# TensorE's program filled up to whole blocks of 256 instructions in every pair of heads, with the first pair and one transposition in another order

## The reference

```
x = x + attention(layernorm(x), ctx)      # 32 heads of 128, additive position bias, mask over keys
x = x + ffn(layernorm(x))                 # base linear + LoRA of 8 experts weighted by a softmax router
attention: q = xn @ Wq; k = ctx @ Wk; v = ctx @ Wv            # 1024 x 512 by 512 x 4096 each
           p = softmax(q k^T / sqrt(128) + bias, masked)      # per batch and head, 64 x 64
           out = concat(p v) @ Wo                             # 1024 x 4096 by 4096 x 512
```

## Time and profile before

| | us |
|---|---|
| three runs | 796.79, 797.21, 797.59 (median 797.21) |
| profiled execution | 795.04 |
| its span | 793.3 |
| TensorE busy | 778.4 |
| VectorE (DVE) busy | 523.3 |
| ScalarE (ACT) busy | 399.9 |
| GpSimd (POOL) busy | 184.9 |

### The profile page before, as it was taken

The page is one execution under the profiler, slowest core; times in us unless marked ns, Lnnn a source line. Parts: engine busy times, 40 slices in busy tenths (PEclk is TensorE's granted clock), DMA queues, the critical chain, the costliest instruction groups (busy, mean ns, idle before and its releaser), DMA issues.

```text
span 793.3 us, 16707 instructions
## 1 busy us (share of the span) xinstructions
PE 778.4 (98%) x6360; PEld 652.7 (82%) x6360; DVE 523.3 (66%) x951; ACT 399.9 (50%) x1138; POOL 184.9 (23%) x203
## 2 busy tenths in 40 slices
PE   9999999999999999889999999999999999999998
PEld 7888888888888888768888888888888888887886
DVE  6883626267677666477767776677667676657974
ACT  5663525245555555555664466545654466436520
POOL 0225041033433334232211221212211221000200
PEclk9999999999999999999999999999999999999999
DMA  6536773244645547473563356435553455442002
GB/s 226 198 121 220 224 247 135 110 137 159 193 162 157 179 143 225 155 233 118 160 183 112 107 164 183 130 113 159 161 164 117 120 160 175 109 115 85 1 5 103
DMA packets 108077, 118.38 MB, mean 149 GB/s; under 512 B 44239, under 2 KB 77007, under 8 KB 107998
## 3 DMA queue, kind: packets, MB, share of 16 engines
q1 hardware_dynamic: 107998, 117.31, 47.4%
HBM read 81.64 MB, written 35.65 MB: 148 GB/s over the span
## 4 chain that ended last, share of the span: by engine, by line
PE 95%; DVE 2%; issue 1%; ACT 1%; DMA 0%; ACTq 0%
PE pY L1391 42%; PE pP L1391 40%; PE pY L1547 4%; PE pO L1572 2%; PE pT_ L1572 1%; PE pO L1391 1%; PE pT_ L1557 1%; PE pS L1557 1%; PE pS L1572 1%; ACT pr L757 1%; DVE st L977 1%; PE pS L1437 0%; PE pO L1437 0%; DVE y L1126 0%; PE pY L1464 0%
## 5 line engine op out<-in xcount | busy, mean ns | idle before, releaser
L757 ACT ACTIVATE pr<-pr,mx 128x64 f32<-128x64 f32 x256 | 86.2, 343 | 29.7 <-DVE mx L1143 29.7
L1126 DVE TENSOR_TENSOR y<-y,pY 128x512 f32<-128x512 f32 x124 | 84.5, 681 | 23.9 <-PE pY L1391 23.6
L1391 PE MATMUL pY<-wo_hi,oT_hi 128*128 128x512 f32 x248 | 97.0, 391 | 0.5 <-issue 0.5
L1391 PE MATMUL pY<-wo_lo,oT_hi 128*128 128x512 f32 x248 | 96.7, 390 | 0.0
L1391 PE MATMUL pY<-wo_hi,oT_lo 128*128 128x512 f32 x248 | 96.6, 389 | 0.0
L907 DVE TENSOR_TENSOR wk_lo<-wk_raw,wk_hi 128x256 fp32r<-128x256 f32 x96 | 49.3, 514 | 61.6 <-ACT wk_hi L649 60.4
L1391 PE MATMUL pP<-xo_hi,wk_hi 128*128 128x512 f32 x210 | 83.5, 398 | 4.1 <-DVE stage L928 2.1
L649 ACT CAST wk_hi<-twk 128x256 fp32r<-128x256 f32 x128 | 50.8, 409 | 65.1 <-PE pP L1391 54.7
L1391 PE MATMUL pP<-xo_lo,wk_hi 128*128 128x512 f32 x210 | 81.9, 390 | 0.0
L1391 PE MATMUL pP<-xo_hi,wk_lo 128*128 128x512 f32 x210 | 81.9, 390 | 0.0
L582 POOL TENSOR_TENSOR bias<-bias,madd 128x512 f32<-128x512 f32 x32 | 41.1, 1300 | 151.4 <-DMA bias<-in_fside_Bx32xSxS 151.4
(11 more groups left out here) (282 smaller groups left out, 1882.0 us busy)
## 6 DMA issues: line engine op xcount, KB each, us to landing
v_hbm<-stage SPq DMA_DIRECT2D x64, 256.0 KB, 2.3
k_hbm<-stage SPq DMA_DIRECT2D x64, 256.0 KB, 3.6
k<-k_hbm SPq DMA_DIRECT2D x16, 1024.0 KB, 5.3
v<-v_hbm SPq DMA_DIRECT2D x16, 1024.0 KB, 7.0
wk_raw<-in_L_xattn_Wk SPq DMA_DIRECT2D x16, 512.0 KB, 4.5
wo_raw<-in_L_xattn_Wo SPq DMA_DIRECT2D x16, 512.0 KB, 3.6
bias<-in_fside_Bx32xSxS SPq DMA_DIRECT2D x128, 64.0 KB, 3.5
wk_raw<-in_L_xattn_Wq SPq DMA_DIRECT2D x16, 512.0 KB, 4.7
```

Of the source, the lines that this page charges most:

```text
L757: nc.scalar.activation(pr[s][:, b, :], pr[s][:, b, :], ACT.Exp, bias=mx[:, s, b:b + 1], accum_out=sm[:, s, b:b + 1]).then_inc(exp_made, 1)
L1126: nc.vector.tensor_tensor(y[:, t, :], y[:, t, :], src[:, :], ALU.add).then_inc(y_added, 1)
L1391: mm = nc.tensor.matmul(bank_, a, b, start=first and n == 0, stop=last and n == len(terms) - 1, skip_group_check=read_between)
```

## The change

QB = QA + 1 gets a name. Block QB uses the alternating banks too, and the blocks after it use pP. The first products of QB are issued before product 4 of QA, product 1 of block QB + 1 is issued before products 3 and 4 of QB, and ACT's and DVE's programs of this stretch are interleaved to match. In each pair `turn_p(h + 1)` moves behind `scores(h + 2)` and `scores(h + 3)`; in pair NP - 2 it moves behind `scores(h + 2)`. Two alignments are added to TensorE's program. `addr_align(256, offset=k)` makes the loader put idle instructions (NOPs) in front of the next instruction until that one stands k instructions behind a multiple of 256: once in the prelude, before `times(QB + 1, 1)`, with offset 12, and in every pair of the loop, between `times(n, 2)` and `times(n, 6)`, with offset 144.

```diff
+QB = QA + 1
@@ order of the products
-ORDER += [(QA, 3), (QA, 4)]
-for n_ in range(QA + 1, NBLK):
+ORDER += [(QA, 3), (QB, 1), (QA, 4), (QB, 2), (QB, 6), (QB, 7), (QB, 5), (QB + 1, 1), (QB, 3), (QB, 4)]
+ORDER += [(QB + 1, p) for p in (2, 6, 7, 5, 3, 4)]
+for n_ in range(QB + 2, NBLK):
@@ banks (x_bank; y_bank alike)
-            return pP[0] if n > QA else (pP[0], pY[0])[n % 2]
+            return pP[0] if n > QB else (pP[0], pY[0])[n % 2]
@@ ACT, prelude, from the end of copy_v(QA), higher(w, 4)
-            copy_c12(n)
             exp(0, 0)
-            exp(0, 1)
-            higher(w, 5)
-            exp(1, 0)
-            exp(1, 1)
-            higher(w, 6)
...
+            copy_c12(n)
+            higher(w, 5)
+            copy_p1(QB)
+            exp(0, 1)
+            higher(w, 6)
+            exp(1, 0)
+            higher(w2, 0)
+            copy_u(QB)
+            exp(1, 1)
+            higher(w2, 1)
+            higher(w2, 2)
+            copy_v(QB)
...
+            wo_high(0)
+            copy_p1(QB + 1)
+            copy_c12(QB)
...
@@ DVE, prelude
-            make_c22(n)
             largest(0)
             biased(1)
             largest(1)
+            make_c22(n)
...
+            make_c11(QB)
             lower_w(w2, 0)
-            weights(0)
-            weights(1)
             lower_w(w2, 1)
             lower_w(w2, 2)
+            invert(0)
+            weights(0)
+            make_c22(QB)
+            weights(1)
...
@@ TensorE: waits of times for its bank
-                    before = n - 1 if n > QA else n - 2
+                    before = n - 1 if n > QB + 1 else n - 2
+                    if n == QB:
+                        pe.wait_ge(s_read, p)
@@ TensorE: wait of scores(2), scores(3)
-                    pe.wait_ge(s_read, s + 1)
+                    pe.wait_ge(c21_made if s else c12_made, QB + 1)
@@ TensorE: prelude
             times(n, 3)
+            times(QB, 1)
             times(n, 4)
-            for p in (1, 2, 6, 7, 5, 3, 4):
-                times(n + 1, p)
+            for p in (2, 6, 7, 5):
+                times(QB, p)
+            nc.tensor.addr_align(256, offset=12)
+            times(QB + 1, 1)
+            times(QB, 3)
+            times(QB, 4)
@@ TensorE: every pair i of the loop
                 turn_p(h)
-                turn_p(h + 1)
                 scores(h + 2)
                 scores(h + 3)
+                turn_p(h + 1)
                 times_v(h)
                 times_v(h + 1)
-                for p in (1, 2, 6, 7):
+                for p in (1, 2) if i else (2,):
+                    times(n, p)
+                if True:
+                    nc.tensor.addr_align(256, offset=144)
+                for p in (6, 7):
                     times(n, p)
@@ TensorE: pair NP - 2
             turn_p(h)
+            scores(h + 2)
             turn_p(h + 1)
-            scores(h + 2)
```

More of the change, by code:

```diff
@@ L260, in x_bank @@
         def x_bank(n):
-            return pP[0] if n > QA else (pP[0], pY[0])[n % 2]
+            return pP[0] if n > QB else (pP[0], pY[0])[n % 2]
         def y_bank(n):
-            return pP[1] if n > QA else (pP[1], pY[1])[n % 2]
+            return pP[1] if n > QB else (pP[1], pY[1])[n % 2]
         def first_turn(j):
@@ L791, in _ @@
             n, w, late = QA, next_set(QA), late_set(QA)
+            w2 = next_set(QB)
             copy_p1(n)
@@ L802, in _ @@
             higher(w, 4)
-            copy_c12(n)
             exp(0, 0)
-            exp(0, 1)
-            higher(w, 5)
-            exp(1, 0)
-            exp(1, 1)
-            higher(w, 6)
[L811 to L820, removed]
             copy_c12(n)
             higher(w, 5)
+            copy_p1(QB)
+            exp(0, 1)
             higher(w, 6)
+            exp(1, 0)
[5 more added lines that the diff above has]
+            copy_v(QB)
+            higher(w2, 3)
+            higher(w2, 4)
+            wo_high(0)
+            copy_p1(QB + 1)
+            copy_c12(QB)
+            higher(w2, 5)
+            higher(w2, 6)
             def higher_of(w, slot):
@@ L838, in _ @@
                 o_high(h + 1, 0)
-                copy_p1(n)
+                if i:
+                    copy_p1(n)
                 o_high(h + 1, 1)
@@ L1193, in _ @@
             make_c21(n)
-            n, w2 = QA + 1, next_set(QA + 1)
             lower_w(w, 6)
-            make_c11(n)
-            invert(0)
+            make_c11(QB)
             lower_w(w2, 0)
-            weights(0)
-            weights(1)
             lower_w(w2, 1)
             lower_w(w2, 2)
+            invert(0)
+            weights(0)
+            make_c22(QB)
+            weights(1)
             lower_w(w2, 3)
-            make_c22(n)
             lower_w(w2, 4)
             lower_wo(0)
+            make_c21(QB)
             lower_w(w2, 5)
-            make_c21(n)
             lower_w(w2, 6)
@@ L1413, in times @@
                 if p in (1, 2):
-                    before = n - 1 if n > QA else n - 2
-                    if n == 2:
+                    before = n - 1 if n > QB + 1 else n - 2
+                    if n == QB:
+                        pe.wait_ge(s_read, p)
+                    elif n == 2:
                         pe.wait_ge(c12_made if p == 1 else c22_made, 1)
```

## The result

The changed kernel takes 1,011.8 us (median of 6 runs, 1,008.7 to 1,013.8), the kernel before 796.4 (median of 6): ratio 1.2697, 95% interval [1.2676, 1.2718], slower by 215 us. 884 us were predicted, at most 912. The direction was right, the size was not.

The account below looks back on a forecast made before the run. The prediction took TensorE, multiplying for 98% of the span, as the bound. Its terms -3 + 0 + 95 - 5 = +87 us, with 795.0 us profiled and 2.2 us to the median, gave 884 us; the 8-in-10 range was 787 to 912 us.

Parts of the forecast that it names:

- Part 1: First pair's scores, exponentials and block QB interleaved: 3 us gained, out of 3.7 us of waits behind DVE and ACT.
- Part 2: turn_p(h+1) moved behind both scores: taken as nothing; 1 to 4 us over 14 pairs if ACT's copy slips.
- Part 3: Idle instructions of both alignments, 2,612 in all, partly hidden by TensorE's queued work: +95 us.
- c: Sequencer's cost of one idle instruction: 51 ns estimated, with bounds of 7.3 ns and 0.1 us.
- cover: Queued TensorE work hiding the filling: 2.7 us per pair, 1.3 in pair 0, 2 in the prelude; 38 us together.
- Part 4: TensorE's waits at starts of 256-instruction program blocks should go once those starts stand still: 5 us gained, between 0 and 6.5.
- Rival C: Idle stretches also slow TensorE's clock: 1.5 us for each of 14, +21 us, 905 us; chance 0.22.
- A: Idle instructions nearly free, below 10 ns each, so the filling is hidden: 789 us, at best 787; chance 0.27.
- B: Idle instructions cost between 10 and 35 ns each: 812 us at 20 ns, 829 us at 30 ns; chance 0.15.
- D: The filling is not there, or is jumped over: 792 to 797 us; chance 0.03.

Follow-up runs that it names:

- run 1: Changed kernel without both alignments, so the new order alone and no idle instructions: 793.3 us, ratio 0.9969.
- run 8: Kernel before with only the first pair's new order, no filling and the transposition in its old place: 793.8 us, ratio 0.9968.
- run 11: Changed kernel with only the transposition put back to its old place, both fillings kept: 969.7 us, ratio 1.2177.
- Run 5: Changed kernel, but SP issues the load of the next k only when times_v of the even head is done: 968.1 us, ratio 1.2151.
- run 3: Kernel before with the alignment of offset 144 in every pair and nothing reordered: 954.3 us, ratio 1.1973.
- run 4: Changed kernel with its 175 idle instructions per pair split into five groups of 35, and 46 in the prelude: 799.9 us, ratio 1.0043.
- run 6: Kernel of run 1 with 36 idle instructions in each of the 14 pairs at the filling's place: 797.4 us, ratio 1.0016.
- run 7: Kernel of run 1 with 88 idle instructions in each of the 14 pairs at the filling's place: 884.0 us, ratio 1.1111.
- run 2: Changed kernel with the same layout, but max_nops=0, so a jump replaces the idle instructions: 815.4 us, ratio 1.0245.
- run 10: Kernel of run 1 with 596 idle instructions in groups of 31 or 32, in the first and every second pair: 791.5 us, ratio 0.9937.
- run 9: Kernel of run 8 with 596 idle instructions in groups of 31 or 32, in the first and every second pair: 790.6 us, ratio 0.9933.

## Why the prediction was wrong, step by step

**Part 1, the first pair: right.** 3 us were taken of 3.7. The waits of the earlier trace rows are gone, and runs 1 and 8 gain 2.5 and 2.7 us in the whole. In the changed kernel the 8.5 us less of other idle time stand for parts 1 and 4 together, which had 3 + 5 = 8.

**Part 2, the moved transposition: taken at nothing, missed twice.** Alone it costs 0.18 us a pair, within the 1 to 4 us given for a slipping copy, but no slipping copy shows: run 1 has no wait on it. Of the 0.18 us, 0.14 are in the four transpositions into pS, which take 0.58 us in the new place (the chain of a pair above) and 0.44 in the old (run 11). Why they do was not tried. With the filling it costs 42 us (run 11). "No DMA moves" was the wrong sentence. SP issues the k load at the same semaphore as before, but TensorE asks for its next block later against it, and the one packet comes in behind 1 MB. Run 5 shows it.

**Part 3, the filling: this step failed.** The form 2,612 c - cover was right; runs 3, 4, 6 and 7 all follow it. Its term c = 51 ns, taken from the nearest row, the wait instruction, is 75 ns: 2,612 x 0.024 = +63 us. It lay inside the two bounds (7.3 ns and 0.1 us), but the range was cut at 61 ns, by nothing in the trace. The cover is 3.0 us and not 2.7, -4 us over 13 pairs; the 2 us and 1.3 us taken for the prelude and pair 0 measured 1.9 us each.
The Trainium skill (TensorE: Matmul & The Clock Gate, Wait — 56ns, not 53.3ns?) has some 62 ns for a matmul that the sequencer's microcode handles. Taken over to an idle instruction, as the prediction's estimate of +124 us did, it was nearer than the wait's 51 ns; the 75 ns measured decide.

**Part 4, the block starts: half right.** The gaps in times_v went, as predicted; the 0.5 us into pY (L1391, 1), an eighth wait "issue" of the kernel before that the earlier trace rows leave out, is there in run 1 too. That the third block would be hidden behind the first 31 idle instructions was not so: it was there 4.3 us after the filling began (401.7 to 406.0 us) and not 1.2. The 13 stops are 12.17 us in the mean against 10.1 without the stand, 13 x 2.05 = 27 us, and that of pair 0 is 13.67 us against the 12.3 of runs 5 and 11: +28 us.
The Trainium skill (Runtime: NRT & Kernel Launch, Instruction fetch mechanics) has a crossing mostly hidden; with a large load in front of the packet this trace shows 2.1 us of standing still.

**Rival C was not an alternative but an addition.** It was given 1.5 us for each stop, from a slow stretch of 3 us. The trace has 13.7 us at 1.2 GHz in a pair, 5.8 of them with TensorE at work. The busy time rose by 45.0 us; 4.0 of them are there in the order alone (782.4 in run 1, for the transpositions and its own stretch at the lower clock), so it is some 2.7 us for each of 15 stops. The prediction gave the forecast full clock and C the lower one, as if one excluded the other; the rows at the start of the kernel had shown a rested array at half pace and should have gone into the sum itself.

Together: 87 + 63 - 4 + 28 + 45 = 219 us against 217.5 of the two spans. So the forecast failed at three of its terms: c too small, the clock left out of the sum, and the block in the filling put at nothing. Rivals A and B fell with c. D is two cases: without the filling run 1 gives 793.3 us, inside its 792 to 797, and with a jump run 2 gives 815 us, outside.

## What to carry to other kernels

Price an instruction that the sequencer carries out alone by the distance of starts, and compare a group of it with what the engine still has queued: here groups of up to 36 in the pairs were hidden, one of 88 was not, nor was one of 46 in the prelude, and 175 a pair in five groups cost 7 us in all where 175 in one cost 218. A stop of the matrix engine can be paid twice, as idle time and as slow matmuls behind it (here behind every filling that stopped it for 3.5 us or more), so put both into one sum. Before fixing where a block of the program starts, look at which large load the core issues just then.

## What was not expected of the hardware

An idle instruction recorded with 13 ns takes 75 ns of TensorE's sequencer. A jump over 175 places takes the sequencer 4.4 us, a third of what the 175 idle instructions take, and leaves TensorE idle for 1.3 to 1.6 us (run 2); groups of up to 36 idle instructions in the pairs were hidden. A stop of 3.46 us is followed by matmuls at 1.2 GHz. For shorter stops the traces don't agree on a length: behind 1.3 to 1.6 us (run 2), 1.9 us (kernel before) and 3.02 us (run 3) the clock stayed at 1.00; behind 3.13 us (run 2), 2.2 us (run 8), 2.0 us (run 1), 1.9 us (run 10) and once 1.2 us (run 9, at 714 us) it fell to 0.50. A 16 KB packet of the program waits behind a 1 MB load of data, and moving one transposition of 0.6 us was enough to put it there (run 11).
